# Layer 2's selective scan, laid out by state and image instead of by channel

## What is computed

```
xz = x @ in_proj_w; x_ssm, z = halves of xz
u  = silu(depthwise 3x3 conv of x_ssm + conv_b)          # four orders of tokens
dpart, B, C = split(u @ x_proj_w[k])                     # 12, 16, 16 columns
delta = softplus(dpart @ dt_w[k] + 2 * dt_b[k])
state = exp(delta * A_neg[k]) * state + (delta * u) * B  # 192 channels x 16 states
y_k   = sum over the 16 states of state * C, + Ds[k] * u
y = layernorm(y_0 + y_1 + y_2 + y_3) * silu(z);  out = y @ out_w
```

## Time and profile before

| what | value |
|---|---|
| median of three runs | 19111.07 us (19109.79 to 19123.44) |
| profiled execution | 19115.89 us |
| its span, first to last instruction | 19114.2 us |
| mean granted TensorE clock | 0.92 of full |
| layers 0 and 1 with what is ahead of them | 6149.8 us |
| layer 2 | 12022.2 us |
| layer 3 | 942.2 us |

### The profile page before, as it was taken

The page is one execution under the profiler, slowest core; times in us unless marked ns, Lnnn a source line. Parts: engine busy times, 40 slices in busy tenths (PEclk is TensorE's granted clock), DMA queues, the critical chain, the costliest instruction groups (busy, mean ns, idle before and its releaser), DMA issues. The chain is left out here.

```text
span 19114.2 us, 278580 instructions
## 1 busy us (share of the span) xinstructions
PE 14621.5 (76%) x79256; PEld 8486.3 (44%) x79256; DVE 13659.7 (71%) x13058; ACT 9805.9 (51%) x14679; POOL 7607.1 (40%) x4057
## 2 busy tenths in 40 slices
PE   7899898989997677767676776677777667767789
PEld 5666666666665333333233333333333333333367
DVE  5666666666665788778688778688787688787732
ACT  4444444444443566565366556266665356665400
POOL 1000000000000477666366666177666366666500
PEclk9999999999998899999899999899999889999999
DMA  5222222222222000000100000100000100000011
GB/s 122 59 59 59 63 51 62 58 64 56 56 59 67 14 4 1 3 4 13 42 2 3 3 4 1 54 1 3 4 1 3 48 7 4 3 1 3 28 47 40
DMA packets 127667, 562.53 MB, mean 29 GB/s; under 512 B 20988, under 2 KB 81788, under 8 KB 105468
## 3 DMA queue, kind: packets, MB, share of 16 engines
q1 hardware_dynamic: 114780, 470.00, 10.0%
q0 software_dynamic: 12288, 86.71, 2.1%
HBM read 440.00 MB, written 126.27 MB: 30 GB/s over the span
## 5 line engine op out<-in xcount | busy, mean ns | idle before, releaser
L1156 POOL TENSOR_TENSOR L2.u<-L2.u 128x784 f32<-128x784 f32 x3072 | 5656.9, 1849 | 1821.7 <-PE L2.ps L1261 1233.6
L1261 PE MATMUL L2.ps<-L2.u,L2.ident 128*128 128x392 f32 x12288 | 4595.7, 499 | 129.4 <-DVE L2.y L1618 129.4
L1630 DVE TENSOR_TENSOR_SCAN L2.u<-L2.u,L2.state,L2.ps 128x784 f32<-128x784 f32 x2304 | 4163.1, 1834 | 175.5 <-ACT L2.ps L1413 146.9
L1419 ACT COPY L2.u<-L2.ps 128x784 f32<-128x784 f32 x3840 | 3102.9, 808 | 902.7 <-PE L2.ps L1230 895.9
L1230 PE MATMUL L2.ps<-L2.bs,L2.sel 96*128 (+3 forms) x6144 | 1626.8, 352 | 2204.1 <-DVE L2.u L1630 925.5
L1413 ACT ACTIVATE L2.u<-L2.d,L2.nega 128x784 f32<-128x784 f32 x2304 | 2190.7, 951 | 2144.0 <-DVE L2.u L1630 1969.0
L1261 PEld LDWEIGHTS L2.ps<-L2.u,L2.ident 128*128 128x128 f32 x12288 | 2177.5, 192 | 1402.5 <-DVE L2.y L1618 186.1
L1605 DVE TENSOR_TENSOR L2.ps<-L2.ps,L2.du 128x784 f32<-128x784 f32 x2304 | 2215.1, 969 | 719.2 <-PE L2.ps L1230 701.0
L1230 PE MATMUL L2.ps<-L2.cs,L2.sel 96*128 96x392 bf16 (+1 forms) x6144 | 1628.8, 348 | 704.4 <-ACT L2.u L1419 672.3
L1230 PEld LDWEIGHTS L2.ps<-L2.bs,L2.sel 96*128 x6144 | 541.9, 101 | 3067.6 <-issue 2854.6
L1145 POOL TENSOR_TENSOR L2.u<-L2.u,L2.du 128x784 f32<-128x784 f32 x768 | 1410.9, 1837 | 1190.1 <-ACT L2.u L1419 1190.1
(11 more groups left out here) (231 smaller groups left out, 21259.3 us busy)
## 6 DMA issues: line engine op xcount, KB each, us to landing
L0.left<-table SPq DMA_DIRECT2D x48, 1176.0 KB
L0.right<-table SPq DMA_DIRECT2D x48, 1176.0 KB
L1.left<-table SPq DMA_DIRECT2D x48, 1176.0 KB
L1.right<-table SPq DMA_DIRECT2D x48, 1176.0 KB
table<-taps POOLq DMA_DIRECT2D x24, 1176.0 KB, 15.8
L0.wg<-L_w SPq DMA_DIRECT2D x49, 433.5 KB, 3.5
L1.wg<-L_w SPq DMA_DIRECT2D x49, 433.5 KB, 3.5
L0.x_res<-x POOLq DMA_DIRECT2D x8, 2352.0 KB, 13.4
```

The source lines that it names most:

```text
L1156: pool.tensor_tensor(hc[:, n % RING, :], hs[:, n % RING, :], cb[n % RING], ALU.mult)\
L1261: mm = pe.matmul(ps[:, 6 + h, 0:HSPAN], ident[:], hc[:, n % RING, h * HSPAN:(h + 1) * HSPAN], start=(n % STATES == 0), stop=(n % STATES == ...
L1419: act.copy(out.rearrange("p (a n) -> p a n", a=2), ps[:, 4:6, 0:HSPAN]).then_inc(c_out, 1)
L1630: dve.tensor_tensor_scan(hs[:, n % RING, :], a, b, state[:, n:n + 1], ALU.mult, ALU.add).then_inc(scanned, 1)
```

## The change

`scan_layer` is replaced by four stages, each a block of its own.

`decay_tables` makes, from A, a weight table for PE: for each direction, channel and state a column block that multiplies delta by -A. The table has a high and a low part; it is written to HBM.

`prep_layer` does for each pair of images what came before the scan: normalisation, projections, filter taps (now three padded tiles), B and C rows, softplus. It is unrolled over 48 tiles, and runs one tile ahead on ACT and DVE. POOL takes the product delta * u and the low part of delta. It writes to HBM: z, u (`xc`), delta as a high and a low part (`d`), delta * u by spans of 112 tokens (`du`), and the rows of B and C (`bc`). The three-way bfloat16 split is gone.

`scan_layer` now has 16 states x 8 images on the partitions. It goes over 4 directions, 28 spans of 112 tokens and 2 halves of the channels. A half has 12 units of 8 channels. For a unit PE forms delta * A for all states (`spread_decay`: weights of 32 rows x 128 columns per channel, 112 columns each, float32r), ACT takes the exponential within PSUM (`decay`) and puts the state carried from the last span in front of each channel's tokens (`carry`). SP loads delta * u from HBM with each image's row read once for each of the 16 states (`load_du`), POOL multiplies it by B, and DVE scans 8 x 114 elements at once. For every token one matmul with C as its 8 weight columns (one per image, zero elsewhere) sums over the states: `sum_states`, 112 of them for a half, in seven fills of 16, placed in units 3 to 9 of the next half; four tokens go to PSUM partitions 0, 32, 64 and 96. ACT copies the sums to SBUF, and SP stores them as y by token.

`fin_layer` loads the four y, adds them with tokens on the partitions (POOL one of the additions), adds Ds * u by matmuls, takes the layer norm with one statistic per token, transposes back on PE, and applies the gate and the output projection.

```diff
--- before.py
+++ after.py
...
-def scan_layer(nc, sems, tag, x_in, x_out, ap, z_dram, consts):
...
+def decay_tables(nc, sems, tag, ap, wa_dram):
...
+def prep_layer(nc, sems, tag, x_in, ap, z_dram, xc_dram, d_dram, du_dram, bc_dram, consts):
...
+            def store_tile(pr, j):
+                k, i = divmod(j, 3)
+                n = pr * TILES + j
+                for half in range(2):
+                    q = 4 * n + 2 * half + 2
+                    span = slice(half * HPIECE, (half + 1) * HPIECE)
+                    sp.wait_ge(d_step, 2 * q)
+                    for at, b, g, jj, size in set_runs(pr, i):
+                        sp.dma_start(d_dram[k, g, 0, b, jj:jj + size, span], hi[at:at + size, span].bitcast(F32))\
+                            .then_inc(hi_stored[half], 16)
+                    sp.wait_ge(du_done, q)
+                    for at, b, c, size in runs(pr, i):
+                        spans = slice(half * NSPANS // 2, (half + 1) * NSPANS // 2)
+                        sp.dma_start(du_dram[k, b, spans, c:c + size, :].rearrange("s c t -> c s t"),
+                                     one[n % 2][at:at + size, span].rearrange("p (s t) -> p s t", t=SPAN))\
+                            .then_inc(du_stored[n % 2][half], 16)
+                    sp.wait_ge(lo_done, q)
+                    for at, b, g, jj, size in set_runs(pr, i):
+                        sp.dma_start(d_dram[k, g, 1, b, jj:jj + size, span], d[n % 2][at:at + size, span])\
+                            .then_inc(lo_stored[n % 2][half], 16)
...
+                        pool.wait_ge(d_step, 8 * n + 2 * q + 1)
+                        pool.tensor_tensor(out, d_q, u_k[:, rows, :], ALU.mult).then_inc(du_done, 1)
+                        pool.wait_ge(d_step, 8 * n + 2 * q + 2)
+                        pool.wait_ge(du_done, 4 * n + q + 1)
+                        pool.tensor_tensor(d[n % 2][:, piece(q)].bitcast(F32R), d[n % 2][:, piece(q)],
+                                           hi[:, piece(q)].bitcast(F32), ALU.subtract).then_inc(lo_done, 1)
...
+                    o_q, e_q, d_q = (v[:, piece(q)] for v in (one[n % 2], e, d[n % 2]))
+                    dve.wait_ge(sp_done, 12 * n + 3 * q + 3)
+                    if n >= 2 and q % 2 == 0:
+                        dve.wait_ge(du_stored[n % 2][q // 2], du_stores(n, 2))
+                    dve.tensor_scalar(o_q, e_q, 1.0, None, ALU.add).then_inc(s_step, 1)
+                    dve.wait_ge(s_step, 12 * n + 3 * q + 1)
+                    dve.scalar_tensor_tensor(out=e_q, in0=o_q, scalar=-1.0, in1=e_q, op0=ALU.add,
+                                             op1=ALU.subtract).then_inc(s_step, 1)
+                    dve.wait_ge(s_step, 12 * n + 3 * q + 2)
+                    dve.tensor_tensor(d_q, d_q, e_q, ALU.subtract).then_inc(s_step, 1)
+            def finish(pr, j):
+                n = pr * TILES + j
+                for q in range(4):
+                    o_q, d_q = (v[n % 2][:, piece(q)] for v in (one, d))
+                    dve.wait_ge(ln_done, 4 * n + q + 1)
+                    dve.wait_ge(s_step, 12 * n + 3 * q + 3)
+                    dve.scalar_tensor_tensor(out=d_q, in0=o_q, scalar=ln1[:], in1=d_q, op0=ALU.subtract,
+                                             op1=ALU.add).then_inc(d_step, 1)
+                    dve.wait_ge(d_step, 8 * n + 2 * q + 1)
+                    if n and q % 2 == 0:
+                        dve.wait_ge(hi_stored[q // 2], d_stores(n))
+                        dve.wait_ge(lo_done, 4 * (n - 1) + q + 2)
+                    dve.tensor_copy(hi[:, piece(q)], d_q).then_inc(d_step, 1)
...
+def scan_layer(nc, sems, tag, wa_dram, d_dram, du_dram, bc_dram, y_dram):
...
+        RA, RB, RD = 3, 3, 6
+        FILLS = 7
+        FROWS = SPAN // 4 // FILLS
+        FIRST_FILL = 3
+        HALVES = 2 * NSPANS
+        h = m.sb("h", [128, 2, HALF, ROW])
+        dm = m.sb("dm", [128, 2, HSET, SPAN], F32R)
+        wa = m.sb("wa", [128, SET, 128], F32R)
+        bt = m.sb("bt", [128, 2, SPAN])
+        cd = m.sb("cd", [128, 2, BATCH, SPAN])
+        du = m.sb("du", [128, RD, UNIT * SPAN])
+        db = m.sb("db", [128, RB, UNIT, ROW])
+        ysum = m.sb("ysum", [128, 2, SPAN // 4, HALF])
+        zero = m.sb("zero", [128, UNIT])
+        ps = m.ps("ps", [128, 8, BANK])
+        decays = [ps[:, 2 * r:2 * r + 2, :].rearrange("p a n -> p (a n)")[:, 0:UNIT * ROW] for r in range(RA)]
...
+            def load_dm(k, s, half, part):
+                g, a = part // 2, part % 2
+                at = 32 * g + 16 * a
+                src = d_dram[k, g].rearrange("q b j t -> (q b) j t")[:, half * HSET:(half + 1) * HSET, span_of(s)]
+                sp.dma_start(dm[at:at + 16, half, :, :].bitcast(F32), src).then_inc(dm_in[half], 16)
+            def load_bt(k, s, half):
+                sp.dma_start(bt[:, half, :], bc_dram[0, k].rearrange("n b t -> (n b) t")[:, span_of(s)])\
+                    .then_inc(bt_in[half], 16)
+            def load_cd(k, s, half):
+                for b in range(BATCH):
+                    sp.dma_start(cd[b:128:BATCH, half, b, :], bc_dram[1, k, :, b, span_of(s)]).then_inc(cd_in[half], 16)
+            def load_du(k, s, half, u):
+                c = u // 3 * SET + half * HSET + u % 3 * UNIT
+                row = du_dram[k, :, s, c:c + UNIT, :] if isinstance(s, int) else \
+                    du_dram[k, :, bass.ds(s, 1), c:c + UNIT, :].rearrange("b a c t -> b (a c) t")
+                row = row.rearrange("b c t -> b (c t)")
+                src = bass.AP(tensor=row.tensor, offset=row.offset,
+                              ap=[[0, STATES], list(row.ap[0]), list(row.ap[1])])
+                sp.dma_start(du[:, (half * UNITS + u) % RD, :], src).then_inc(du_in[(half * UNITS + u) % RD], 16)
+            def store_y(k, s, half):
+                for q in range(4):
+                    at = s * SPAN + SPAN // 4 * q
+                    if k % 2:
+                        at = at * -1 + (TOK - SPAN // 4)
+                    rows = slice(at, at + SPAN // 4) if isinstance(s, int) else bass.ds(at, SPAN // 4)
+                    place = y_dram[k, :, rows, half * HALF:(half + 1) * HALF]
+                    sp.dma_start(place, ysum[32 * q:32 * q + BATCH, half, :, :]).then_inc(y_stored[half], 16)
...
+                    row = bt[:, half, :].unsqueeze(1).to_broadcast([128, UNIT, SPAN])
+                    for u in range(UNITS):
+                        n = half * UNITS + u
+                        pool.wait_ge(du_in[n % RD], loads + 16 * (n // RD + 1))
+                        pool.wait_ge(scanned, units + (n + 1))
+                        pool.tensor_tensor(db[:, n % RB, :, 2:ROW],
+                                           du[:, n % RD, :].rearrange("p (c t) -> p c t", t=SPAN), row, ALU.mult)\
+                            .then_inc(b_ready, 1)
...
+            def spread_decay(k, half, u, units):
+                g = u // 3
+                rows = slice(32 * g, 32 * g + 32)
+                n = half * UNITS + u
+                pe.wait_ge(scanned, units + (n + 1))
+                for e in range(UNIT):
+                    j = half * HSET + u % 3 * UNIT + e
+                    lo, hi = e * ROW + 2, (e + 1) * ROW
+                    for a, b in [(lo, hi)] if hi <= BANK or lo >= BANK else [(lo, BANK), (BANK, hi)]:
+                        mm = pe.matmul(decays[n % RA][:, a:b], wa[rows, j, :],
+                                       dm[rows, half, u % 3 * UNIT + e, a - lo:b - lo], start=True, stop=True)
+                mm.then_inc(d_ready, 1)
+            def sum_states(half, f, fills):
+                bank = 6 + (half * FILLS + f) % 2
+                pe.wait_ge(sum_out, fills + (f + 1))
+                for i in range(FROWS):
+                    for q in range(4):
+                        t = SPAN // 4 * q + FROWS * f + i
+                        mm = pe.matmul(ps[32 * q:32 * q + BATCH, bank, i * HALF:(i + 1) * HALF], cd[:, half, :, t],
+                                       h[:, half, :, 2 + t], start=True, stop=True)
+                mm.then_inc(sum_ready, 1)
...
+                for u in range(UNITS):
+                    spread_decay(k, half, u, units)
+                    f = u - FIRST_FILL
+                    if 0 <= f < FILLS and not first:
+                        if f == 0:
+                            pe.wait_ge(scanned, units + (half * UNITS + RB))
+                            pe.wait_ge(cd_in[1 - half], count(pe, k, s, 128, 128 * half))
+                        sum_states(1 - half, f, before)
...
+            def decay(n, units):
+                act.wait_ge(d_ready, units + (n + 1))
+                a = decays[n % RA].rearrange("p (c t) -> p c t", t=ROW)[:, :, 2:ROW]
+                act.activation(a, a, ACT.Exp).then_inc(a_ready, 1)
+            def carry(half, u, units, first):
+                n = half * UNITS + u
+                act.wait_ge(scanned, units + (n + 1))
```

(27 more changed lines are left out.)

1383 lines of the change are left out of this document (722 added, 661 removed).

## The result

| | us |
|---|---|
| before, median of 4 runs | 19110.4 (19107.9 to 19123.4) |
| after, median of 4 runs | 20632.1 (20626.7 to 20641.4) |
| ratio | 1.0795, 95% interval 1.0777 to 1.0814 |
| forecast | 16750 (15000 to 19200) |

The change makes the kernel 8% slower, where 12% faster was forecast. First the stages of the profile after, by their windows: preparation, scan, gate and output (columns: stretch and its length, busy time of each engine with the number of its instructions, granted clock of PE as a share of full, DMA share, GB/s).

A forecast was written before the change was run, and what follows sets the result against it. DVE bounds the old scan, DMA the new one. Untouched layers 7092, tables 90, preparation 2330, scan 6560, gate and output 620, stage changes 45, plus 2 around it: about 16750 us (15000 to 19200).

The forecast's parts named there:

- Preparation: prep_layer, 4 pairs x 12 tiles: 30 us a tile, 2330 us in all (1750 to 2500).
- DVE and POOL taking turns: Preparation: the two engines do not overlap, so 16 + 14.4 = 30 us a tile.
- the group of four sums: Scan, PE: four sum matmuls to different output quarters take 0.40 us; over 0.7 us would show the prediction wrong.
- 7.34 MB per half span at 252 GB/s: 29 us: Scan, DMA: all transfers at the rate of load bursts; DMA comes last, 224 x 29 = 6500 us.
- SP issues 33 transfers ... 20 us, hidden: Scan, SP: issues at 0.6 us each take 20 us a half span, hidden under DMA's 29.
- PE's 27 us: Scan, PE: decays and sums, 7 x 2.6 + 5 x 2.03 less 1.5 of lead, close behind DMA's 29.
- decays of 1.0 a unit: Scan, PE: nine float32r matmuls of 112 columns at 110 ns each, 1.0 us a unit (0.55 to 1.7).
- the 190 that the prediction named as a sign of being wrong: Scan, PE: float32r matmuls of 112 columns taking over 190 ns (four passes) would show the prediction wrong.
- The point where the change stops paying: Scan: the change loses from 39.2 us a half span on.
- 22 us a chunk: Gate and output: 5.5 MB at 252 GB/s, above DVE's 14 us; 28 chunks make 620 us (480 to 750).
- Rival 3: Scan loads: repeated reads of the same rows are slow, under 187 GB/s the change loses; slow form's chance 0.09.
- Rival 2: Scan, PE: four column tiles do not overlap, 51 us a half span, 21700 us in all; slow form's chance 0.12.

The follow-up runs named there:

- the last trace: Profile of the kernel after with spread delta loads, early gate and output loads, C loads by ACT, and y stores later, one a unit: 17131 us.
- the best kernel: Kernel after with spread delta loads, early gate and output loads, C loads by ACT, and y stores later, one a unit: 17131 us, 0.896 of before.

## Why the prediction was wrong

**What held.** Preparation: 2379 for 2330, with DVE and POOL taking turns as argued; beside POOL's two operations a step of DVE that takes 1.03 us alone took 2.62, and a cast 2.09 for 0.57. A tile took 33 to 37 us for 30, part of it DVE's waits for ACT (532 us in all), which the sum had put at nothing:

```profile
6999.22 1.03 DVE L1296 SCALAR_TENSOR_TENSOR L2p.work<-L2p.work,L2p.ln 128x784 f32<-128x784 f32 x1
7000.28 0.57 DVE L1302 CAST L2p.hi<-L2p.work 128x784 fp32r<-128x784 f32 x1
7000.77 2.62 DVE L1296 SCALAR_TENSOR_TENSOR L2p.work<-L2p.work,L2p.ln 128x784 f32<-128x784 f32 x1
7003.42 2.09 DVE L1302 CAST L2p.hi<-L2p.work 128x784 fp32r<-128x784 f32 x1
```

The scan instruction (2.06 for 2.03), POOL's product (2.08 for 1.99), the group of four sums (0.41 for 0.40), the bytes (170 GB/s x 43.3 us = 7.36 MB for 7.34), and that a load would be what comes last in the scan.

**The step that failed: "7.34 MB per half span at 252 GB/s: 29 us", with "SP issues 33 transfers ... 20 us, hidden".** One rate, read from long bursts over all partitions, was put on four kinds of transfer. From 43.5 us a half span the runs take away, each on top of the last: joined delta rows 0.9 (100 us in all, the preparation being 85 longer); delta over all partitions 7.4 (1666 us); C loads out of SP's row 3.8 (857); y stores spaced and later 1.1 (253). That is 13.2 of the 14.5 us that the forecast lacked, and the last trace shows 30.2. So the 29 us were nearly attained with these bytes, by transfers of another shape and order. For SP's queue the sum was wrong twice: 20 us were 40.9 in the kernel after, and it treated issues as hidden if their sum is, but eight in a row hold up the load behind them whatever the sum.

**A second term, hidden behind the first.** PE's 27 us held decays of 1.0 a unit. They took 21.0 us a half span (195 ns a matmul, just over the 190 that the prediction named as a sign of being wrong), more than half of them at the lower clock (an estimate: 21.0 / 12 = 1.75 a unit lies between 1.21 and 2.16), and 18.1 (4051.5 / 224) in the best kernel at a clock of 0.77; with the sums' 11.5 that is 32.5 and 29.6. So at 29 us of transfers PE would have been level with them, as it nearly is in the last trace. The point where the change stops paying, worked out again from the forecast's own terms, is (19111 - 10190 - 60) / 224 = 39.6 us and not 39.2 (10190 is the forecast without the scan, 60 the scan's starts); it changes no conclusion.

**Gate and output** (1349 for 620): 22 us a chunk was the time of its transfers, and their hiding was taken from two buffers being there. The order in SP's program kept them from being hidden: each chunk waited for loads that were issued too late. With the loads moved, the stage takes 719.

**The rivals.** Rival 3 gave the size almost rightly (its slow form under 187 GB/s, "at 150 GB/s a half span is 49 us") for the wrong reason: rows that repeat run at 381 GB/s. Rival 2 did not occur. The 0.09 on rival 3 was too little for another reason: the delta loads to 16 partitions were in the sum, in one rate with the rest, and no row of before showed a transfer of that shape. The range should have had an unknown there, with both ends.
